# A new order of the work between two attentions of a fused block of transformer layers

## The reference

```python
x = x + 0.5 * ffn(_layernorm(x), w_router, w_block)
x = x + attn(_layernorm(x), Wq, Wk_down, Wv_down, q_to_latent, v_up, Wout)
x = x + 0.5 * ffn(_layernorm(x), w_router, w_block)

def ffn(x):      # 768 of 1024 tokens
    scores = x @ w_router;  top = top_k(scores, 768)
    return x with x[top] replaced by gelu(x[top] @ w_block)

def attn(h):     # 16 heads of 32, latent width 64, causal
    Q = h @ Wq.T;  lk = h @ Wk_down.T;  lv = h @ Wv_down.T
    logits = (Q_head @ q_to_latent[head]) @ lk.T / 8, masked below the diagonal
    return concat(softmax(logits) @ lv @ v_up[head]) @ Wout.T
```

## Time and profile before

| | |
|---|---|
| median of 3 runs | 2931.93 us (2928.39 to 2932.7) |
| profiled execution | 2924.28 us, its span 2922.6 us |
| TensorE busy | 2422.7 us (83%) |
| VectorE busy | 1732.3 us (59%) |
| ScalarE busy | 1160.9 us (40%) |
| mean granted clock of TensorE | 0.938 |

### The profile page before, as it was taken

How to read it: one execution, slowest core, us unless ns; L and a number is a source line. 1 busy time by engine, 2 the same in 40 slices (tenths; PEclk the granted TensorE clock), 3 DMA queues, 4 the chain that set the end, 5 groups by cost and what they waited for, 6 DMA issues and landing times.

```text
span 2922.6 us, 53539 instructions
## 1 busy us (share of the span) xinstructions
PE 2422.7 (83%) x21888; PEld 1499.6 (51%) x21888; DVE 1732.3 (59%) x4806; ACT 1160.9 (40%) x2057; POOL 402.2 (14%) x510
## 2 busy tenths in 40 slices
PE   3868887988879988788887988879888898879887
PEld 2634465544655446544565445654455544555445
DVE  3557635776367753677447764467645776457735
ACT  3314533345333454244432453324533345333442
POOL 0101111101011111011110111111111111111021
PEclk9969999999999999999999999989999999999998
DMA  3100011100111002010010101101011010101000
GB/s 137 58 1 2 2 58 58 59 2 2 60 57 59 2 2 87 30 59 2 16 72 29 60 2 44 58 21 54 2 44 72 20 41 2 58 29 59 2 2 29
DMA packets 42482, 106.19 MB, mean 36 GB/s; under 512 B 2432, under 2 KB 3968, under 8 KB 38400
## 3 DMA queue, kind: packets, MB, share of 16 engines
q1 hardware_dynamic: 42240, 102.77, 9.8%
HBM read 64.49 MB, written 37.75 MB: 35 GB/s over the span
## 4 chain that ended last, share of the span: by engine, by line
PE 58%; DVE 19%; ACT 9%; issue 9%; POOL 3%; DMA 0%; SPq 0%; DVEq 0%; POOLq 0%; ACTq 0%
PE psum L663 25%; PE psum L676 14%; PE psum L789 6%; PE psum L782 6%; DVE psum L917 5%; DVE part L915 3%; PE psum L679 3%; PE psum L690 3%; ACT pr L644 2%; ACT nt_h L566 2%; ACT norm L585 2%; DVE junk L867 2%; PE psum L705 2%; DVE junk L865 2%; POOL x L545 1%
## 5 line engine op out<-in xcount | busy, mean ns | idle before, releaser
L644 ACT ACTIVATE pr<-psum 128x512 f32<-128x512 f32 x1152 | 617.5, 597 | 700.4 <-PE psum L679 700.4
L917 DVE CUSTOM_DVE_ANT_0 psum<-psum,mask_b 128x512 f32<-128x512 f32 (+3 forms) x1024 | 473.7, 524 | 262.2 <-PE psum L690 259.8
L676 PE MATMUL psum<-qk,qk 32*128 32x512 f32 (+3 forms) x4608 | 518.6, 372 | 120.6 <-DVE part L915 57.3
L690 PE MATMUL psum<-qk,qk 32*128 32x512 f32 (+3 forms) x4608 | 525.1, 380 | 41.2 <-DVE part L915 22.1
L676 PEld LDWEIGHTS psum<-qk,qk 32*128 32x128 f32 x4608 | 324.6, 188 | 449.0 <-DVE part L915 181.3
L915 DVE TENSOR_REDUCE part<-psum 128x1 f32<-128x512 f32 x512 | 326.4, 685 | 131.8 <-PE psum L690 131.8
L690 PEld LDWEIGHTS psum<-qk,qk 32*128 32x128 f32 x4608 | 319.4, 193 | 70.0 <-DVE part L915 28.9
L782 PE MATMUL psum<-pr,v_sb 128*32 128x512 f32 (+3 forms) x3072 | 317.9, 509 | 23.9 <-POOL pr L558 22.3
L789 PE MATMUL psum<-pr,ones 128*32 128x512 f32 (+3 forms) x3072 | 320.4, 513 | 0.0
L558 POOL TENSOR_SCALAR_AFFINE_SELECT pr<-pr 128x512 f32<-128x512 f32 x256 | 158.3, 636 | 1096.5 <-ACT pr L644 1096.5
L705 PE MATMUL psum<-ident,norm 128*128 128x128 f32 x768 | 128.2, 300 | 124.3 <-ACT norm L585 122.4
(11 more groups left out here) (115 smaller groups left out, 3461.0 us busy)
## 6 DMA issues: line engine op xcount, KB each, us to landing
x<-x_dram SPq DMA_DIRECT2D x16, 1024.0 KB, 6.7
spill_x<-x SPq DMA_DIRECT2D x16, 1024.0 KB, 4.3
x<-spill_x SPq DMA_DIRECT2D x16, 1024.0 KB, 5.6
out_dram<-x SPq DMA_DIRECT2D x16, 1024.0 KB, 5.1
w_h<-scratch_o SPq DMA_DIRECT2D x7, 1024.0 KB, 4.8
w_l<-scratch_o SPq DMA_DIRECT2D x7, 1024.0 KB, 7.1
w_h<-scratch_q SPq DMA_DIRECT2D x6, 1024.0 KB, 4.8
w_l<-scratch_q SPq DMA_DIRECT2D x6, 1024.0 KB, 6.9
```

The lines of the kernel that those rows point to most:

```text
L644: nc.scalar.activation(pr_of(b, g, u)[:, 2 * p + place, :], bank(e, place), ACT.Exp, scale=SCALE).then_inc(exp_ready, 1)
L676: eng.matmul(o, (k_h, k_h, k_l)[t][own, P * j:P * (j + 1)], (q_h, q_l, q_h)[t][own, queries], start=(t == 0 and at == 0), stop=False, skip ...
L690: m = eng.matmul(bank(e, place)[:, at:at + w], (q_h, q_h, q_l)[t][own, P * i:P * (i + 1)], (k_h, k_l, k_h)[t][own, BANK * block:BANK * blo ...
L917: m = nc.vector.tensor_tensor_reduce(scores, scores, mask_b[:, BANK - w:BANK], 1.0, FAR, ALU.add, ALU.max, top_of)
```

## The change

- In the last group of an attention the next batch's first norm is written out, one T in each of the first eight units, NO two tiles ahead, and SC after units 4 and 8. Its first two NO lie at the end of the third group. SCOL, RT, RF and GX leave the attention.
- In `project`, SCOL follows F 0, two RT follow each of F 1 to F 4, and RF and the GX come after the F tiles. Each CB is followed by its ST. CB therefore waits for the routes of its own batch.
- The last sums of attention b (`left`, four pieces) come between T 0 to T 3 of the second norm. T 4 to T 7 come between the four Q of half 0. The loads XR or XL come right behind LAT 1.
- K and V are spread: two pairs, one pair and one pair ahead of the Q of half 1, and the last four pairs behind. MX units 0 to 4 of the next group 0 lie behind the Q of half 1 and between the last K and V, and take banks of ring G.
- In `back`, ST follows each O, MX units 5 to 8, MC and XT have fixed places, T 0 and T 1 follow O 6 and O 7, T 4 to T 7 lie between F tiles, SC 1 after F 2, SCOL after F 3, and two RT after each of F 4 to F 7.
- HS of half 0 waits for the Q of half 0 alone, no longer for the last Q.

```diff
@@ -100,53 +100,64 @@
 def program_order():
 
 
...
+    def stats(s, b, i):
+        return [("ST", s, b, i)]
+    def scales(s, b, c):
+        return [("VA", s, b, c), ("RS", s, b, c), ("NM", s, b, c)]
+    def front(b):
+        out = []
+        for c in range(NC):
+            for i in range(TC * c, TC * (c + 1)):
+                out += stats(0, b, i)
+            out += scales(0, b, c)
+        out += [("NO", 0, b, 0), ("NO", 0, b, 1)]
+        for i in range(NT):
+            out += [("T", 0, b, i)] + ([("NO", 0, b, i + 2)] if i + 2 < NT else [])
+            out += [("SC", 0, b, i // TC)] if i % TC == TC - 1 else []
         return out
 
...
+    def project(b, left):
+        out = [("F", 0, b, 0), ("G", 0, b, 0), ("SCOL", 0, b)]
+        for i in range(1, NT):
+            out += [("F", 0, b, i), ("G", 0, b, i)]
+            out += [("RT", 0, b, 2 * (i - 1)), ("RT", 0, b, 2 * i - 1)] if i <= TC else []
+        out += [("RF", 0, b)] + [("GX", 0, b, i) for i in range(NT)]
+        for c in range(NC):
+            for i in range(TC * c, TC * (c + 1)):
+                out += [("CB", 0, b, i)] + stats(1, b, i)
+            out += scales(1, b, c)
+        out += [("NO", 1, b, 0), ("NO", 1, b, 1)]
+        for i in range(TC):
+            out += [("T", 1, b, i)] + ([("NO", 1, b, i + 2)] if i + 2 < TC else []) + (left[i] if left else [])
+        out += [("LAT", b, 0), ("XS", b, 0), ("NO", 1, b, TC), ("NO", 1, b, TC + 1)]
+        for i in range(TC, NT):
+            out += [("Q", b, i - TC, 0), ("T", 1, b, i)] + ([("NO", 1, b, i + 2)] if i + 2 < NT else [])
+        out += [("LAT", b, 1), ("XS", b, 1)]
+        out += [("XR", b - 1, 0), ("XR", b - 1, 1)] if b else [("XL", 1, 0), ("XL", 1, 1)]
+        splits = [[("HS", b - 1, g, c)] if b else [] for c in range(NC) for g in range(NQ)]
+        keys = [[("K", b, n // NC, n % NC), ("V", b, n)] for n in range(NT)]
+        for n in range(NQ):
+            out += (keys[0] + splits[0] + keys[1] + splits[1] if n == 0 else keys[n + 1] + splits[n + 1] if n < 3 else [])
+            out += [("Q", b, n, 1)] + (maxima(b, 0, n) if n < 3 else [])
+        out += [("W2", b - 1, "o")] if b else []
+        out += maxima(b, 0, 3)
+        for n in range(TC, NT):
+            out += keys[n] + splits[n] + (maxima(b, 0, 4) if n == TC + 1 else [])
         return out
 
...
+    def maxima(b, g, u):
+        return [("MX", b, g, u, 0), ("MX", b, g, u, 1)]
+    def gathered(b, g, c):
+        return [("MC", b, g, c)]
+    def turned(b, g, c):
+        return [("XT", b, g, c)]
 
     def attention(b):
 
@@ -164,12 +175,6 @@
             g, u = units[n]
             return [(b, g + 1, c) for c in range(NC) if LAST[c] == u] if g + 1 < NQ else []
 
...
         def mask(n):
             g, u = units[n]
             return [("AM", b, g, c, j) for c, j in SCORES[u] if diagonal(c, j)]
@@ -188,19 +193,42 @@
         for n in range(len(units)):
             g = units[n][0]
             groups[g].append(combined(n, 0) + (values(n - 2) if n >= 2 else []))
-            groups[g].append(combined(n, 1) + mask(n) + gathered(n) + (turned(n - 1) if n else []) + (sums(n - 2) if n >= 2 else []))
+            groups[g].append(combined(n, 1) + mask(n) + [("MC", *e) for e in closes(n)]
+                             + ([("XT", *e) for e in closes(n - 1)] if n else []) + (sums(n - 2) if n >= 2 else []))
         last = len(units) - 1
-        groups[-1].append(values(last - 1) + sums(last - 1) + values(last) + sums(last))
-        return groups
+        return groups, [values(last - 1), sums(last - 1), values(last), sums(last)]
 
     def back(b):
...
+        beside = b + 1 < B
+        def more(u):
+            return maxima(b + 1, 0, u) if beside else []
+        out = []
         for i in range(NT):
-            out += [[("F", 1, b, i), ("G", 1, b, i), ("RT", 1, b, i)]]
+            out += [("O", b, i)] + stats(2, b, i)
+            if i == 1:
+                out += more(5)
+            if i == 3:
+                out += scales(2, b, 0) + more(6)
+            if i == 4 and beside:
+                out += gathered(b + 1, 0, 1)
+            if i == 5:
+                out += [("NO", 2, b, 0), ("NO", 2, b, 1)] + (turned(b + 1, 0, 1) if beside else []) + more(7)
+            if i >= 6:
+                out += [("T", 2, b, i - 6), ("NO", 2, b, i - 4)]
+        out += ([("W2", b + 2, "q")] if b + 2 < B else []) + scales(2, b, 1) + more(8)
+        out += [("T", 2, b, 2), ("T", 2, b, 3)] + (gathered(b + 1, 0, 0) if beside else [])
+        out += [("SC", 1, b, 0), ("NO", 2, b, 4), ("NO", 2, b, 5)] + (turned(b + 1, 0, 0) if beside else [])
+        def layer(i):
+            return [("F", 1, b, i), ("G", 1, b, i)]
+        out += layer(0) + [("T", 2, b, 4), ("NO", 2, b, 6), ("T", 2, b, 5), ("NO", 2, b, 7)]
+        out += layer(1) + [("T", 2, b, 6), ("T", 2, b, 7)] + layer(2) + [("SC", 1, b, 1)] + layer(3) + [("SCOL", 1, b)]
+        for i in range(TC, NT):
+            out += layer(i) + [("RT", 1, b, 2 * (i - TC)), ("RT", 1, b, 2 * (i - TC) + 1)]
         return out
 
     def ending(b):
@@ -209,29 +237,28 @@
         out[-1] += [("OUT", b, 1)]
         return out
 
-    sched = [("XL", 0, 0), ("XL", 0, 1)] + norms(0, 0, 0) + norms(0, 0, 1) + sum(front(0), []) + project(0)
-    sched += sum(maxima(0, 0), [])
+    sched = [("XL", 0, 0), ("XL", 0, 1)] + front(0) + project(0, None)
+    for u in range(5, UNITS):
+        sched += maxima(0, 0, u) + sum([gathered(0, 0, c) + turned(0, 0, c) for c in range(NC) if LAST[c] == u], [])
     for b in range(B):
...
+        groups, left = attention(b)
+        if b > 0:
+            tail = ending(b - 1)
+            tail.append([("XL", b + 1, c) for c in range(NC)] if b + 1 < B else [("XR", b, c) for c in range(NC)])
+            groups[0] = [weave(groups[0], tail, 0, len(groups[0]) // 2)]
         if b + 1 < B:
-            sched += project(b + 1)
-            sched += weave(back(b), maxima(b + 1, 0), 1, len(back(b)))
+            ahead = [[e] for c in range(NC) for i in range(TC * c, TC * (c + 1))
+                     for e in stats(0, b + 1, i) + (scales(0, b + 1, c) if i % TC == TC - 1 else [])]
+            groups[2] = [weave(groups[2], ahead, 0, len(groups[2]))] + [[("NO", 0, b + 1, 0), ("NO", 0, b + 1, 1)]]
+            for u in range(UNITS):
+                groups[3][2 * u] += [("T", 0, b + 1, u)] if u < NT else []
+                groups[3][2 * u + 1] += [("NO", 0, b + 1, u + 2)] if u + 2 < NT else []
+                groups[3][2 * u + 1] += [("SC", 0, b + 1, u // TC - 1)] if u in (TC, NT) else []
+        sched += sum(sum(groups, []), [])
+        if b + 1 < B:
+            sched += project(b + 1, left) + back(b)
         else:
-            sched += [("HS", b, g, c) for c in range(NC) for g in range(NQ)] + sum(back(b), []) + sum(ending(b), [])
+            sched += sum(left, []) + [("HS", b, g, c) for c in range(NC) for g in range(NQ)] + back(b) + sum(ending(b), [])
     beside, taken = {}, set()
     for e, after in zip(sched, sched[1:]):
         if e not in taken and e[0] in ("S", "MX") and after[0] in ("S", "MX") and (e[0] != after[0] or e[:4] == after[:4]):
@@ -273,7 +300,8 @@
         if e in beside_of:
             continue
         if k in ("S", "MX"):
-            own = take("N", 0, 4, 4) if k == beside[e][0] else take("A", 0, 6, 4)
+            early = k == "MX" and e[2] == 0 and e[3] <= 4
+            own = take("G", 0, 6, 4) if early else take("N", 0, 4, 4) if k == beside[e][0] else take("A", 0, 6, 4)
             banks[e], banks[beside[e]] = own[1::2], own[0::2]
         elif k == "XT":
             own = banks[e] = take("N", 0, 4, 1) if e[2] == 0 else take("A", 0, 6, 1)
@@ -629,7 +657,7 @@
                 elif k == "HS":
                     b, g, c = e[1:]
                     act.wait_ge(heads_ready, nth["HE", b, NQ - 1, 0])
-                    act.wait_ge(q_done, nth["Q", min(b + 1, B - 1), NQ - 1, NC - 1])
+                    act.wait_ge(q_done, nth["Q", min(b + 1, B - 1), NQ - 1, c])
                     copy(nt_of(2, b)[0][:, g, c * BANK:(c + 1) * BANK], ht[:, g, c * BANK:(c + 1) * BANK]).then_inc(hsh_ready, 1)
                 elif k == "S":
                     b, g, u, p = e[1:]
```

More of the change, by code:

```diff
@@ L100, in program_order @@
 def program_order():
-    def norms(s, b, c):
-        return [("ST", s, b, i) for i in range(TC * c, TC * (c + 1))] + [("VA", s, b, c), ("RS", s, b, c), ("NM", s, b, c)]
-    def turns(s, b, c):
-        tiles = list(range(TC * c, TC * (c + 1)))
-        out = [[("NO", s, b, tiles[0]), ("NO", s, b, tiles[1]), ("T", s, b, tiles[0])]]
-        for n in range(1, TC):
-            ahead = [("NO", s, b, tiles[n + 1])] if n + 1 < TC else []
-            out.append(ahead + [("T", s, b, tiles[n])])
-        return out
@@ L114, in routes @@
-    def routes(f, b):
-        return [[("RT", f, b, i)] for i in range(NT)] + [[("RF", f, b)]] + [[("GX", f, b, i)] for i in range(NT)]
-    def front(b):
```

(47 more changed lines are left out.)

15 lines of the change are left out of this document (removed).

## The result

The changed kernel takes 2803.02 us (median of 4 runs, 2796.58 to 2809.85), the kernel before 2931.39 in the same session: a ratio of 0.956, 95% interval 0.954 to 0.958, so 128 us less. Forecast were 2765, in a range from 2705 to 2850: the right sign, 38 us too optimistic. The span of the profiled execution fell from 2922.6 to 2794.9 us.

What follows compares the result with a forecast made beforehand. No engine bounds throughout: TensorE paces where fed, elsewhere chains of small steps. Seven passes save 22 each (154), head 13.5, tail loses 1: 166.5 off 2924.3 gives 2757.8; medians run 7.6 higher, so 2765 us, range 2705 to 2850.

Steps and rivals of the forecast that it cites:

- G3: Last attention group with the next front pass woven in: 37.6 us forecast, against 57.9 before with the last sums.
- P1: F tiles to the first LAT: 40.0 us forecast, against 29.6 before; the route chain now stands open.
- LAT 1 to O 0: From LAT 1 through Q, K, V and early maxima to the first output projection: 30.8 us forecast.
- B: Output projection, third norm and second feed-forward: 72.6 us forecast including 2.0 charged for late first scores, against 85.5 before.
- The bound at full clock, 37.6: F 0 to LAT 0 if the clock stays at 2.4 GHz: 37.6 us, the lower end kept beside 40.0.
- The rule cited there: Between F and LAT 0: a wait between matmul bursts throttles the next burst every repetition; 40.0 us, without it 37.6.
- four of the six banks are held by MX until VectorE has reduced them: In the K, V, Q turns after LAT 1: 4.4 us of work takes 4.6 to 5.5 a turn.
- V did wait on VectorE: Sign of being wrong, K stage: V and O waiting long on VectorE; no size given.
- tiles cost about 0.1 in six units and 0.5 in the first two: Last attention group: eight transpose tiles among its units add 1.2 us.
- (a): Rival, whole pass: chain and VectorE's queue run later, each pass gives back 15 of its 22; 2870 us, 6 in 100.
- (b): Rival, wait in the second norm through output projection: clock stays at 1.2 GHz; 3030 us, 5 in 100.
- (c): Rival: clock holds from F through second feed-forward, VectorE's lateness absorbed in the attention; 2720 us, 12 in 100.

Runs made afterwards that it cites:

- experiments 1: Kernel before with only the new last group and the new order up to LAT 0, old order behind it: 2872.2 us, ratio 0.980.
- experiment 3: Changed kernel with the last sums back at the end of the attention, ahead of F 0: 2850.3 us, ratio 0.973.
- experiment 2: Changed kernel with maxima units 0 to 4 of batches 1 to 7 back among the output projections: 2877.7 us, ratio 0.983.
- experiment 5: Changed kernel with SCOL ahead of F 0 instead of behind it: 2786.6 us, ratio 0.951.
- Experiment 9: Changed kernel with new bank order, SCOL ahead of F 0, and third norm's T 2 and T 3 ahead of its second scales: 2712.1 us, ratio 0.926.
- experiment 4: Changed kernel with the four banks of an early MX pair dealt in the order VectorE frees them: 2793.5 us, ratio 0.953.

## Why the prediction was right, and where it was off

The means of the seven passes, against the forecast for each stage:

| stage | before | forecast | after |
|---|---|---|---|
| G3 | 57.2 | 37.6 | 40.1 |
| P1 | 29.8 | 40.0 | 38.5 |
| LAT 0 to LAT 1 | 17.1 | 17.4 | 17.4 |
| LAT 1 to O 0 | 30.9 | 30.8 | 34.6 |
| B, to the first scores | 86.4 | 70.6 | 71.7 |
| first head group | 42.0 | 44.0 | 44.5 |

**The mechanisms held.** The gain is the order's: routes under F instead of under the attention (4.5 us a pass by experiments 1 and 3), last sums in a hole (6.2, experiment 3), maxima beside Q and K instead of packed between the output projections (10.7, experiment 2). The prices overlap, as each edit was taken from the whole; the tiles between F tiles were not tried alone. P1 loses, as said, and the route chain sets where its second norm starts (experiment 5). The chain had the length of batch 0's, as the prediction took it: gain done 18.4 us after F 0, eight GX in 7.94. GX slows CB and not the statistics between:

```profile
1377.23 1.18 DVE L916 SCALAR_TENSOR_TENSOR x<-nt_act,sel,x 128x512 f32<-128x512 f32 x1 [0.98 <-POOL x L573]
1378.45 0.69 DVE L861 BATCH_NORM_STATS2 stats<-x 128x6 f32<-128x512 f32 x1
...
1388.32 0.73 DVE L916 SCALAR_TENSOR_TENSOR x<-nt_act,sel,x 128x512 f32<-128x512 f32 x1
1389.09 0.69 DVE L861 BATCH_NORM_STATS2 stats<-x 128x6 f32<-128x512 f32 x1
```

Beside GX, CB takes 1.18, 0.78, 1.12 and 0.74 us, and 0.73 to 0.75 after it; the statistics take 0.69 each time. The Trainium skill ("GPSIMD Engine Reference", section "1. Specifications") says that GpSimd shares its SBUF interfaces with VectorE and contends with instructions that have two SBUF inputs; CB has two, the statistics one, so the trace agrees.

**P1, too high by 1.5.** The prediction let the last sums run wholly at the lower clock (8.4 in place of 4.2 us). The clock did fall in every pass, during the wait of 5.2 to 5.5 us ahead of T 0, but the low stretch was over before LAT 0, and sums and four tiles together took 9.2 us in the pass shown. The bound at full clock, 37.6, was the better value: P1 lasted 37.9 in the pass where it was shortest. (Its own terms give 35.0+4x0.6 = 37.4. In the trace NM ends at 35.3 and the four low halves take 2.7.) The rule cited there from the Trainium skill ("TensorE: Matmul & The Clock Gate", section "HAM oscillation — how this bites in real kernels"), that a wait throttles what follows in every repetition, is borne out that far: the granted clock over P1 is 0.91 or 0.96, never 1.00, in all seven passes. What failed was the price that the prediction put on it, a low stretch as long as the sums and tiles. With the wait halved to 2.4 to 2.7 us the clock over P1 was 0.95 in nine passes of experiments 5 and 9 and 1.00 in five.

**LAT 1 to O 0, too low by 3.8.** The step "four of the six banks are held by MX until VectorE has reduced them" was right, and the sizes of the turns, 4.6 to 5.5 us, were not: I let the next Q have a bank after the first reduction. By the ring it gets the one that VectorE frees third. The four waits on `part` are 3.7 us; without them the stage got 2.0 shorter on average, and 2.6 from shortest pass to shortest pass (experiment 4). What stays over the forecast is a wait of 1.0 for a V's copy on ScalarE and, in some passes, the clock; neither was tried by itself. V did wait on VectorE, which the prediction had as a sign of being wrong if it were long; it was 0.8 to 1.0 us, twice a pass.

**G3, too low by 2.5.** The step "tiles cost about 0.1 in six units and 0.5 in the first two" put 1.2 us on eight tiles. They took 2.5. A unit takes 3.7 us, where it was 3.45: behind the values the tile starts after 1.00 us, where the sums started after 0.88, the sums too take 1.00, and the wait for the scores is gone. That PV and DEN take so long there was read from the trace and not tried apart. With 2.9 in place of 2.8 for each SC this makes 39.1, the length of three passes. The mean is 1.0 more: three passes have a wait of 1.4 us ahead of an XT early in the group, which batch 7, from which the forecast was made, does not have; one of them has a clock of 0.96 as well, and a fourth waits 0.7 ahead of F 0.

**B, too low by 1.1; the first group 0.5.** (The terms of B add up to 70.2, not 70.6, so they were 1.5 too low.) O 0 to SC 0 took 39.0 where 37.7 were forecast, and the rest 32.7 where the terms give 32.5. In the three passes in which the clock up to SC 0 was 0.95 or 0.96 it took 37.5 or 37.6, as forecast. In the other four a low stretch among the output projections comes on top (0.88 to 0.93). The wait ahead of SC 0 was 5.6 in all seven. The prediction had no low stretch there.

**How the misses add up.** The stages are 5.9 us a pass over the forecast and the next group 0.5, 6.5 without rounding. The forecast had left 1.0 of them for the clock: it took 22 a pass off the mean of 221.4, which is 199.4, and the stage sum is 198.4. So 5.4 a pass, 38 in all. The head gave 12.0 (forecast 13.5), the tail lost 0.4 (forecast 1). That is 38.8 for the profiled execution, 2796.6 against 2757.8. P1 was wrong in the other direction from the rest; without that luck the miss would be 10 us more.

Of the rivals, (a) is the one that took a share: VectorE's queue and the clock give back more than I stepped. (b) fell: the mean granted clock rose from 0.938 to 0.946. (c) did not happen in this kernel. Experiment 9 reaches its time with three small edits of the order (2712 us, forecast 2720) and clocks of 0.95 to 1.00 in P1 and 0.97 to 1.00 in B, but its other half, that VectorE's lateness is absorbed, did not come: the first group still takes 44.2.

## What to carry to other kernels

When a list is the order of every engine's queue, step each engine through it and note what stands in front of the one small result that the array waits for; here a variance, a power and a maxima unit in front of two tile halves cost 57 us of 2803. A wait of TensorE is worth more than its length if dense work at the lower clock follows it, and work that fits in a hole is worth more than its own time for the same reason. When a ring of buffers is handed to several engines, deal it in the order in which they are freed.
